# The second layer's products, weighed on ScalarE and added on GpSimd instead of combined on VectorE

## The reference

```python
x = x + _L0_attn_ref(_L0_cond_ref(x, cond_1024, ...), ...)   # LSTM over time, then causal attention
x = x + _L0_ffn_ref(_L0_cond2_ref(x, cond_1024, ...), ...)   # GRU over time, then mixture of experts
```

```python
top_w, top_i = jax.lax.top_k(probs, 2)
h = jax.nn.gelu(jnp.einsum('td,ndh->tnh', xt, w1) + b1, approximate=False)
out_all = jnp.einsum('tnh,nhd->tnd', h, w2) + b2
sel = jnp.take_along_axis(out_all, top_i[:, :, None], axis=1)
out = (sel * top_w[:, :, None]).sum(axis=1)
```

## Time and profile before

| | |
|---|---|
| Median of 3 runs | 571.53 us (571.21 to 572.6) |
| The profiled execution's own time | 572.81 us |
| Its span in the trace | 571.0 us |
| Mean granted clock of TensorE | 0.955 of full speed |

### The profile page before, as it was taken

How to read it: one execution, slowest core, us unless ns; L and a number is a source line. 1 busy time by engine, 2 the same in 40 slices (tenths; PEclk the granted TensorE clock), 3 DMA queues, 4 the chain that set the end, 5 groups by cost and what they waited for, 6 DMA issues and landing times.

```text
span 571.0 us, 20274 instructions
## 1 busy us (share of the span) xinstructions
PE 529.1 (93%) x7418; PEld 481.5 (84%) x7418; DVE 416.5 (73%) x2338; ACT 350.9 (61%) x1297; POOL 32.3 (6%) x85
## 2 busy tenths in 40 slices
PE   8979889799789999999999999999999998989998
PEld 3746676788779999999999999999999998879998
DVE  4446778878767888888888888888888796855342
ACT  2225545876256676767676767676767676566572
POOL 6000000000000000000000000000000000000000
PEclk9789959999658999999999999999999999999999
DMA  7810101010000101010101010101011010100000
GB/s 209 339 16 6 20 2 17 5 15 15 10 11 7 17 3 20 13 21 2 21 12 20 3 18 14 17 7 14 15 15 12 12 15 14 14 2 1 13 7 10
DMA packets 75119, 14.34 MB, mean 25 GB/s; under 512 B 71411, under 2 KB 74111, under 8 KB 74638
## 3 DMA queue, kind: packets, MB, share of 16 engines
q1 hardware_dynamic: 74566, 11.96, 11.5%
q10 hardware_dynamic: 456, 1.08, 0.6%
HBM read 7.78 MB, written 1.05 MB: 15 GB/s over the span
## 4 chain that ended last, share of the span: by engine, by line
PE 67%; DVE 18%; ACT 8%; issue 6%; SPq 0%; DMA 0%; DVEq 0%; ACTq 0%
PE pH L488 16%; PE pG L488 11%; PE pY L488 11%; PE pL L488 8%; PE pV L488 7%; PE pC L580 6%; PE pS L488 5%; ACT hid L870 4%; PE pC L488 3%; DVE latNlo L988 2%; DVE gB L1149 2%; DVE ghi L1152 2%; DVE glo L1155 1%; ACT gC L892 1%; DVE acc L1083 1%
## 5 line engine op out<-in xcount | busy, mean ns | idle before, releaser
L870 ACT ACTIVATE hid<-pH,b 128x256 f32<-128x256 f32 (+1 forms) x320 | 115.2, 437 | 4.2 <-PE pH L488 4.2
L488 PE MATMUL pY<-w,hid 128*128 128x128 f32 x608 | 84.2, 281 | 0.0
L488 PE MATMUL pH<-ghi,w1hi 128*128 128x256 f16 (+1 forms) x320 | 75.6, 252 | 4.5 <-issue 2.8
L488 PE MATMUL pH<-ghi,w1lo 128*128 128x256 f16 (+1 forms) x320 | 75.8, 253 | 0.0
L488 PE MATMUL pH<-glo,w1hi 128*128 128x256 f16 (+1 forms) x320 | 75.8, 252 | 0.0
L488 PEld LDWEIGHTS pY<-w,hid 128*128 128x128 f32 x608 | 73.7, 191 | 0.2
L877 ACT ACTIVATE gT<-pG 128x32 f32<-128x32 f32 x128 | 24.8, 194 | 71.3 <-PE pG L488 70.7
L488 PE MATMUL pG<-gRZ,gW 128*128 128x16 f32 x256 | 45.9, 255 | 7.7 <-DVE gRZ L1134 7.6
L1149 DVE TENSOR_TENSOR gB<-gRZ,gC 128x16 f32<-128x16 f32 x128 | 22.4, 175 | 41.2 <-ACT gC L892 40.0
L488 PEld LDWEIGHTS pG<-gRZ,gW 128*128 128x128 f32 x256 | 40.7, 199 | 12.6 <-DVE gRZ L1134 11.8
L859 ACT ACTIVATE PThi<-pC 128x512 f16<-128x512 f32 x64 | 38.1, 596 | 21.0 <-PE pC L580 21.0
(11 more groups left out here) (181 smaller groups left out, 1636.2 us busy)
## 6 DMA issues: line engine op xcount, KB each, us to landing
w<-in_w SPq DMA_DIRECT2D x2, 2048.0 KB, 13.0
qbd<-qh SPq DMA_DIRECT2D x256, 16.0 KB, 1.9
out<-acc SPq DMA_DIRECT2D x16, 64.0 KB, 1.5
xT<-in_xT ACTq DMA_DIRECT2D x1, 960.0 KB, 7.7
hid<-in_WqT SPq DMA_DIRECT2D x1, 512.0 KB, 5.3
hid<-in_Wout SPq DMA_DIRECT2D x1, 512.0 KB, 9.7
lWh<-in_lWh SPq DMA_DIRECT2D x1, 256.0 KB, 2.8
lWx<-in_lWx SPq DMA_DIRECT2D x1, 256.0 KB, 3.1
```

Source lines behind the costliest of these rows:

```text
L488: return nc.tensor.matmul(o, lhsT=lhsT, rhs=rhs, start=start, stop=stop, skip_group_check=True)
L870: A(hid[:, e % NHID, c, 0:W], pH[half][:, W * at:W * (at + 1)], ACT.Gelu, bias=b1[:, e, c:c + 1], scale=1.0 / SP).then_inc(gelu, 1)
```

## The change

VectorE's `combine` is gone. ScalarE gets `scale_down`: for each product it does one activation (Copy, with the gate as a scale read from SBUF) from the PSUM bank into a small SBUF buffer `part`, and counts a new semaphore `scaled`. `part` has two places, one for slot A and one for slot B; before a place is written again, ScalarE waits until GpSimd has used it. GpSimd gets a `combine` that waits for `scaled` and adds `part` to `acc`. TensorE now waits on `scaled` where it waited on `acc_done` to write a bank again; its own instructions and their order are the same. SyncE still waits on `acc_done`.

The places on ScalarE: slot B of step k - 1 is scaled in step k directly behind `gT`. Slot A of step k is scaled near the end of step k, behind `lC`, and ahead of `th`.

```diff
--- before.py
+++ after.py
@@ tensors, semaphores @@
+        part = sb('part', [128, 2, 2, D])
+        scaled = sem("scaled")
+        SLOTS = "AB"
@@ gpsimd @@
+            def combine(k, slot):
+                for at, (m, e, tg) in enumerate(DOWN_AT[(k, slot)]):
+                    pool.wait_ge(scaled, ORDER[(m, e, tg)] + 1)
+                    if e == 0:
+                        pool.wait_ge(r_copy, 2 * (TILES[m][tg] + 1))
+                    else:
+                        pool.wait_ge(acc_done, ORDER[(m, e - 1, tg)] + 1)
+                    pool.tensor_tensor(acc[:, m % 3, tg, :], acc[:, m % 3, tg, :], part[:, SLOTS.index(slot), at, :], ALU.add).then_inc(acc_done, 1)
+
             for k in range(STEPS):
                 if latents_at(k) is not None:
                     split_latents(latents_at(k))
+                if (k, "A") in DOWN_AT:
+                    combine(k, "A")
+                if (k, "B") in DOWN_AT:
+                    combine(k, "B")
                 if k in FIRST:
                     rank_experts(FIRST[k])
@@ tensor: lat_q, turn_probs, values, route_x, experts_down @@
                 if downs_before(k, "C"):
-                    pe.wait_ge(acc_done, downs_before(k, "C"))
+                    pe.wait_ge(scaled, downs_before(k, "C"))
...
@@ scalar @@
+            def scale_down(k, slot):
+                act.wait_ge(down_mm, ORDER[DOWN_AT[(k, slot)][-1]] + 1)
+                before = [ORDER[d] for (j, sl), ds in DOWN_AT.items() if sl == slot and j < k for d in ds]
+                if before:
+                    act.wait_ge(acc_done, max(before) + 1)
+                for at, (m, e, tg) in enumerate(DOWN_AT[(k, slot)]):
+                    if e == 0:
+                        i = TILES[m][tg]
+                        act.wait_ge(route[i % 2], 10 * (i // 2 + 1))
+                    A(part[:, SLOTS.index(slot), at, :], bank_of(k, slot)[:, D * at:D * (at + 1)], ACT.Copy,
+                      scale=gates[:, m % 3, tg, e:e + 1]).then_inc(scaled, 1)
...
                     A(gT[:, :, :], pG[:, 0:2, g % GS, :], ACT.Tanh, scale=1.0 / SP).then_inc(g_tanh, 1)
+                if (k - 1, "B") in DOWN_AT:
+                    scale_down(k - 1, "B")
                 if k >= LAG:
                     setup(k)
...
                     exps(unit_at(k - 1, O_S))
+                if (k, "A") in DOWN_AT:
+                    scale_down(k, "A")
                 if k < LAG:
                     setup(k)
...
+            scale_down(STEPS - 1, "B")
@@ vector @@
-            def combine(k, slot):
...
-                if (k, "A") in DOWN_AT:
-                    combine(k, "A")
...
-                if (k - 1, "B") in DOWN_AT:
-                    combine(k - 1, "B")
...
-            combine(STEPS - 1, "B")
```

More of the change, by code:

```diff
@@ L532, in lat_q @@
                 if downs_before(k, "Y"):
-                    pe.wait_ge(acc_done, downs_before(k, "Y"))
+                    pe.wait_ge(scaled, downs_before(k, "Y"))
                 if G:
@@ L594, in values @@
                 if downs_before(k, "V"):
-                    pe.wait_ge(acc_done, downs_before(k, "V"))
+                    pe.wait_ge(scaled, downs_before(k, "V"))
                 copied(k)
@@ L656, in route_x @@
                 if downs_before(k + 1, "V"):
-                    pe.wait_ge(acc_done, downs_before(k + 1, "V"))
+                    pe.wait_ge(scaled, downs_before(k + 1, "V"))
                 mm(pV[:, 256:256 + E], flat(g8[:, GS * n:GS * (n + 1), :]), gateW[:, :], start=True)
@@ L688, in experts_down @@
                         if downs_before(k, bank):
-                            pe.wait_ge(acc_done, downs_before(k, bank))
+                            pe.wait_ge(scaled, downs_before(k, bank))
                         if bank == "V":
```

## The result

| | before | changed |
|---|---|---|
| Median of 4 runs each | 571.47 us (571.21 to 572.6) | 579.9 us (576.39 to 580.75) |
| Ratio, with its 95% interval | | 1.0135 (1.0104 to 1.0166) |
| Same, second chip session (17 and 6 runs) | 573.33 us | 578.9 us, 1.0095 (1.0068 to 1.0122) |
| The profiled execution's own time | 572.81 us | 580.32 us |
| Span in the trace | 571.0 us | 578.5 us |

A forecast was written before the change was run, and what follows sets the result against it. It took TensorE (busy 529.1 of 571.0 us) as the bound, with ScalarE pacing it at the Gelus. Terms 4.7 + 0 - 0.5 + 0.3 + 0.55 = +5.0 on 572.81 gave 577.8, median 576.5; range 575 to 578.5, 8 in 10 572.5 to 580.5.

The forecast's parts named there:

- Product ahead of the Gelus: Steps 55 to 135 (11 places) and 139 to 145 (7): Gelus and TensorE's pH product 0.26 later each, 4.7 us.
- Steps 74 to 76: In each 8 steps `gRZ` comes 0.37 earlier, given back at step 76's transposes: 0, between -3.7 and +3 in all.
- rival D: GpSimd's additions and VectorE block each other, 0.44 us at two places per 8 steps: 8.8 more, 585 us; chance 0.04.
- Steps 133 to 135: After the LSTM, two combinations leave VectorE's chain and ScalarE's products stand in idle time: -0.5 us.
- Step 151: TensorE's pV product waits for slot A of step 150, scaled on ScalarE behind 8 Gelus: +0.3 us.
- The end: Last product: 0.92 us through ScalarE and GpSimd in place of 0.35 on VectorE, +0.55 us.
- the signs that I named: Among them: step 140's Gelus 0.36 behind `gT`, `gRZ` wait in step 75 below 0.1, step 76's transposes waiting about 0.4.
- the signs of being wrong: Steps 139 to 145 keep their length, step 76's transposes don't wait, or GpSimd's additions lengthen VectorE's small operations.
- A: At step 75 and its like VectorE's relief reaches TensorE in full, -3.7: +1.3, 572.8 us; chance 0.12.
- B: Insertion ahead of the Gelus almost free, 0.10 per place, and the relief arrives: -1.6, 570.0 us; chance 0.05.
- C: TensorE's half-clock stretch at 150 to 155 us goes, -3.9, 572.6 us, or comes later at the same cost; chance 0.07.
- E: Products behind `lC` gate TensorE by the upper bound of 0.3 us in 10 places: 579.5 us; chance 0.10.

The follow-up runs named there:

- slot A alone: Against the kernel before, only slot A's products go by ScalarE and GpSimd, slot B's stay combined on VectorE: 571.12 us, ratio 0.9974.
- relief only: The kernel before with only slot A of steps 34, 50, 58, ... 130 and slot B of steps 132 and 133 moved: 567.47 us, ratio 0.9937.

## Why the prediction was right, and where its sizes were off

Slower, as forecast. The measured 579.9 lies in the range for 8 in 10 (572.5 to 580.5), near its upper end, and above the forecast's own range (575 to 578.5). Against the profiled execution I forecast +5.0 us, it was +7.5, of which 1.3 stand ahead of step 50 and are chance in the main. The second session's +5.6 is closer to the forecast than the steps are: there it was +6.2. Term by term, from the shifts of `gT`:

- **Product ahead of the Gelus**, forecast 18 x 0.26 = 4.7: 16 jumps of 0.26 and one of 0.17, 4.33. Right, in mechanism and size. Missed was only step 127, where nothing is lost: TensorE waits there for the Gelus of half 1 behind it, before and after (0.95, then 0.69 us), and that wait takes the 0.26. I had carried step 79 over to all eleven like it without reading each.
- **Steps 74 to 76**, forecast 0: +1.10 over ten patterns. The give-back came as told, and the run with slot A alone shows it alone. What failed is the step "so `gRZ` comes about 0.37 earlier". Reckoned from `gT`, it came 0.06 earlier. A part is size: the place of the 0.35 us combination is worth 0.25, since it overlaps its neighbours (from the start of `gates` to that of the transpose it is 0.51 with it and 0.26 without), and 0.25 is what arrives with slot A alone. The other 0.2 are mechanism. In their place stands GpSimd's addition, which stretches `hlo`. That is rival D, which I had at 0.04 because one `hlo` in the earlier trace rows kept 0.18 us beside an operation of GpSimd. The row was a coincidence: `hlo` ended at 281.71, 0.03 behind the end of that operation (281.68), which is just where a held one ends. And "This trace does not show it" was a wrong reading: the trace of the kernel before has it at four places, `hfull` and `gA` in steps 28 and 44 (at 98 and 160 us), beside GpSimd's ranking. VectorE, then GpSimd, in step 44:

```profile
160.17 0.33 DVE L1170 TENSOR_TENSOR hfull<-oK,lC 128x16 f32<-128x16 f32 x1
```

```profile
160.14 0.32 POOL L473 TENSOR_TENSOR eq<-eq,tri 128x64 f32<-128x64 f32 x1 [14.36 <-DVE gt L1042]
```

`hfull` takes 0.33 where 0.17 is usual and ends 0.03 behind `eq`. The Trainium skill's rule (page "SBUF — State Buffer", section "Who interferes with whom") on an exclusive lock, which I had cited and set aside, is what the runs here agree with. The price is the overlap that is left, 0.14 to 0.3 us, and not the 0.44 that I reckoned for D.

- **Step 110**, not forecast: +0.38, cause open.
- **Steps 133 to 135**, forecast -0.5: -0.61.
- **Step 151**, forecast +0.3: +0.39. TensorE's product at 562.34 in the earlier trace rows starts at 569.31, 6.97 later, and the shift ahead of it was 6.31 + 0.26.
- **The end**, forecast +0.55: +0.54.

The sum is 4.33 + 1.10 + 0.38 - 0.61 + 0.39 + 0.54 = 6.13, of the 6.18 measured from step 50. The forecast of +5.0 came within 1.1 us of it partly by luck: 1.48 us that it did not have stand against about 0.4 that it had too much.

Of the signs that I named, steps 139 to 145 and step 79 came as told (0.35 from `gT` to the Gelus, 0.26 longer, 0.10 behind them). The wait for `gRZ` did not fall below 0.1, it was 0.47; the wait ahead of the transposes was 0.20, not 0.4. And one of the signs of being wrong came true: the additions on GpSimd did make VectorE's small operations longer. That VectorE's busy time would fall by 44 us and ScalarE's rise by 40 to 48 was wrong too, it was 25.7 and 28.8: instructions that overlap their neighbours leave, or bring, less than their durations. GpSimd's 58 was as told. Two readings were loose. The rows did not agree with an addition at twice VectorE's time, only with the direction: 441 ns against 345 is 1.28 times, and the change's additions took 460. And by the chances of the rivals themselves "same" has 0.18 and "faster" about 0.03, not 0.14 and 0.07; nothing rests on that.

Rivals A and B needed the relief to arrive and stay. In the changed kernel 0 to 0.15 arrives, and with slot A alone 0.25, of which 0.18 is given back. B also needed a place that costs less than 0.15. Of C the traces say that the half-clock stretches vary between programs and runs; the changed kernel even shows one more, at 115 to 120 us (the third figure from the end is the granted clock, here a mix of its levels 1.00 and 0.50, 2.4 and 1.2 GHz; it was 1.00 there before), and none was shown to follow from the change. E's wait is there too, 0.15 to 0.23 at steps 53, 61, ... 125; with the bit of relief ahead of it, 0.1 for each 8 steps is left, not 0.3.

```profile
115.00:120.00 5.00, 5.00 (x89) 4.94 (x89) 2.15 (x17) 2.45 (x11) 0.72 (x2) 0.74 0.02 3
```

## What to carry to other kernels

Before work is given to an idle engine, read the order around the place where it goes: before the change ScalarE was idle for 39% of the span, and a product put ahead of the Gelus still cost TensorE its full 0.26 us at 16 of 18 places, while the same product in the idle time ahead of `PThi`, in steps 77 and 78, cost nothing. Move only the instructions whose engine is waited for just then: 14 of 128 products moved gained 3.7 us from step 50 on, all 128 lost 6.2. And look for a shared resource in the durations of the neighbours, over many overlaps and by when they end, not in one row.

## What the hardware showed that I had not expected

- A VectorE operation with two SBUF operands that starts within a GpSimd addition of 128x128 does not end before it: where it would, it ends 0.02 to 0.05 us behind it. `hlo` 0.17 becomes 0.32 to 0.47, `hhi` 0.46. The exceptions, 18 in the changed kernel, started within 0.015 us of the addition's own start: they kept their 0.15 to 0.18, and the addition took 0.48 to 0.50 in place of 0.46. At one place `den`, a `tensor_scalar` with a single SBUF operand, was held too (0.34 in place of 0.16). Operations that read PSUM (`mx`, the combination, `lg`) keep their times beside it.
- A Copy of 128x128 on ScalarE holds its place for 0.17 us with a constant scale and 0.25 with a scale per partition; one of 16 columns for 0.07.
- Two gaps of 0.25 to 0.28 us that no wait explains, each at one instruction (VectorE's `PTlo` of step 108 in seven traces, ScalarE's Gelu of step 140 with relief only). What they are stays open.
